# One stream of max units across the blocks of a context attention, its first phase rebuilt, and a lag of two chunks before the probabilities are weighed

## The chip, the cores and the metric

The kernel runs on one core of one Trainium2 chip. The metric is the device time in microseconds of one execution. TensorE (PE) does matrix products into PSUM, VectorE (DVE) and ScalarE (ACT) read PSUM and SBUF, GpSimd (POOL) works on SBUF, and SyncE (SP) issues most DMAs. The engines run on their own and wait for each other through semaphores.

## What is computed

A decoder of two layers on 1024 tokens (8 tiles of 128) of width 128 and a context of 6404 rows. Layer 0 is a state-space mixer (mamba), an attention of 16 heads of size 8 over the context, and a mixture of experts; layer 1 is a self-attention, a second attention over the context and another mixture of experts. After each comes a residual and a layer norm. The change is in layer 0, in its first two parts and the norm between them. The part of the reference that matters most:

```python
def _L0_xattn_ref(q, kv, mem, w_q, w_kv, w_concat):
    B, L, D = q.shape
    c = jnp.concatenate([mem, kv], axis=1)
    qh = (q @ w_q).reshape(B, L, N_HEAD, D_HEAD).transpose(0, 2, 1, 3)
    kvp = c @ w_kv
    k, v = (kvp[..., :D_HEAD], kvp[..., D_HEAD:])
    attn_score = jnp.einsum('bhid,bjd->bhij', qh, k) / np.sqrt(D_HEAD)
    attn_prob = jax.nn.softmax(attn_score, axis=-1)
    out = jnp.einsum('bhij,bjd->bhid', attn_prob, v)
    ...
x = _layernorm(x + _L0_attn_ref(x, ...))            # the mixer
x = _layernorm(x + _L0_xattn_ref(x, ctx_1024, ...)) # the context attention
```

All heads share the keys and values (6404 rows of 8 numbers each), and `softmax` needs for every query the maximum over the 6404 scores.

## The kernel before, in words

`context_attention` works in `NB` = 16 blocks. A block is 8 heads of one tile of 128 tokens, so 1024 queries. Keys are split into parts whose products sum to the wanted precision, and stand in `key_stack` twice, in partitions 0 to 63 and 64 to 127; the queries of even blocks stand in partitions 0 to 63 of `q_stack`, those of odd blocks in 64 to 127. `rows(blk)` picks the half. So a product of block b uses 64 rows of the PE array, the lower or the upper ones by the parity of b.

Each block goes through two passes. The first finds the maxima: 56 **max units** (`UNITS`, 8 heads by 7 ranges of keys). A unit is one or two matmuls of 64 x 512 (line 802; the seventh range of a head is one matmul of 260 columns) into one of two places of `max_ps`, and a reduce on DVE (`maximum`, line 959) that frees the place (`unit_used`). When all units of a block are reduced, `negate` makes two parts of the negated maxima, `turn_shift` turns them on PE (8 transposes, line 815), and a cast writes them as two further rows of `q_stack` (line 971, on DVE); that sets `q_ready`. The second pass goes over 51 **chunks** of 128 keys (`NCH`): two score matmuls (line 922; the shift is in them) into one of three banks, two exponentials on ACT (`exponentiate`, line 950) into `probs`, three deep, and `weigh` on PE (line 903), which multiplies a chunk's probabilities with the values into `acc_ps`. A block's sum is copied by ACT (`take_acc`, line 940) before the next block's first `weigh`.

The order on PE is written out by hand in `attend`. While block b goes through its chunks, PE works off the max units of block b+1, of the other parity:

```python
if with_max and c <= LAST:          # LAST = 46: one unit behind the scores of chunks 0 to 46
    max_unit(pe, blk + 1, u)
weigh(pe, blk, c - 1)               # the chunk before
if with_max and c in after_weighing:  # 9 more: behind chunks 4, 9, 14, 19, 25, 30, 35, 40, 46
    max_unit(pe, blk + 1, u)
if with_max and c == NCH - 2: turn_shift(pe, blk + 1)
```

Before block 0 there is a first phase: 16 query products (line 832), split by ACT and DVE (lines 837 and 841), the 56 max units of block 0, and 27 jobs that make layer 1's keys and values (lines 875 and 880). Ahead of that, in `mamba`, PE also makes the keys and the values of the context (`ContextKeys`): keys are `make` (line 350), values are `values` (line 359, 51 products with 8 columns each, 12 near the start and 39 later), and `take_values` copies them on DVE. `residual_norm` stands between mixer and attention: DVE normalizes, PE transposes 8 tiles (line 196), ACT copies them to `x_T`.

Of the kernel before, what the change touches and what calls it, by code (L numbers as in the profile page):

```python
# [23 lines left out]
P = 128  # L24
# [74 lines left out]
def load_and_constants(k):  # L99
# [8 lines left out]
    k.half_sel_q = k.sb("half_sel_q", [P, 1])  # L108
    k.steps = Chain(None, k.sem("vector_step"))
# [7 lines left out]
    with nc.Block() as block:  # L117
# [8 lines left out]
        def _(dve):  # L126
# [9 lines left out]
            for lo in (TERMS, P // 2 + TERMS):  # L136
                nc.vector.memset(k.half_sel[lo:lo + 32, :], 1.0)
                nc.vector.memset(k.shift_one[lo:lo + 32, :], 1.0)
            nc.vector.tensor_copy(k.ident_b[:], k.ident[:]).then_inc(k.consts_ready, 1)


def residual_norm(k, tag, branch, added=False, store=None, turned=None):
# [5 lines left out]
    with ExitStack() as tmp:  # L148
# [11 lines left out]
        with nc.Block() as block:  # L160
# [21 lines left out]
            def _(act):  # L182
# [101 lines left out]
class ContextKeys:  # L284
# [10 lines left out]
    def __init__(self, k, banks):  # L295
# [6 lines left out]
        self.v_ready, self.v_taken = k.sem("ctx_v_ready"), k.sem("ctx_v_taken")  # L302
# [49 lines left out]
    def values(self, pe, w_kv, chunks):  # L352

        nc, k = self.k.nc, self.k
        for c in chunks:
            n = P if c < NCH - 1 else TAIL
            if c in (0, self.CUT):
                pe.wait_ge(self.ctx_loaded[1 if c else 0], 16)
            ins = nc.tensor.matmul(self.v_ps[0:n, c, :], k.ctx_T[:, c * P:c * P + n], w_kv[:, HD:2 * HD], start=True,
                                   stop=True)  # L360
        if NCH - 1 in chunks:
            ins.then_inc(self.v_ready, 1)
# [36 lines left out]
def mamba(k):  # L399
# [8 lines left out]
    with ctx:  # L408
# [87 lines left out]
        with nc.Block() as block:  # L496
# [54 lines left out]
            def _(pe):  # L551
# [7 lines left out]
                keys.values(pe, w_kv, range(0, 12))  # L559
# [23 lines left out]
                keys.values(pe, w_kv, range(12, NCH))  # L583
# [3 lines left out]
                pe.wait_ge(keys.v_taken, 1)  # L587
# [72 lines left out]
            def _(dve):  # L660
# [36 lines left out]
                keys.take_values(dve)  # L697
# [27 lines left out]
        residual_norm(k, "norm0", out_ps, turned=wide(4))  # L725
# [20 lines left out]
def context_attention(k):  # L746
# [5 lines left out]

# [12 lines left out]
    with ctx:  # L765
        q_stack = k.sb("q_stack", [SPAN2, NT, BLK], F32R, ctx)
        gathered = k.sb("gathered", [P, NB, QUART], F32, ctx)
        w_out = k.params.x0_w_concat
        with ExitStack() as tmp:

            probs = k.sb("probs", [P, 3, BLK], F32, tmp)
            partial = k.sb("max_partial", [P, HB, NR], F32, tmp)
            neg = k.sb("neg_max", [P, HB], F32, tmp)
            part2 = k.sb("neg_part", [P, HB, 2], F32R, tmp)
# [3 lines left out]
            shift_ps = max_ps[:, 0, :]  # L778
            q_made, q_high, q_done = k.sem("q_made"), k.sem("q_high"), k.sem("q_done")
# [7 lines left out]

            def rows(blk):

                lo = HALF_P * (blk % 2)  # L790
                return slice(lo, lo + HALF_P)

            def max_half(pe, blk, u, a):

                h, r = u // NR, u % NR
                c0, cols = RANGES[r]
                n = min(HALF, cols - a)
                if a == 0 and not (blk == 0 and u < 2):
                    pe.wait_ge(unit_used, blk * UNITS + u - 1)
                if n <= 0:  # L800
                    return
                ins = nc.tensor.matmul(max_ps[:, u % 2, a:a + n], q_stack[rows(blk), blk // 2, h * P:(h + 1) * P],  # L802
                                       k.key_stack[rows(blk), c0 + a:c0 + a + n], start=True, stop=True)
                if a + n == cols:
                    ins.then_inc(unit_ready, 1)
# [29 lines left out]
            def high_queries(act, i):  # L835
                act.wait_ge(q_made, i + 1)
                nc.scalar.copy(q_rows(i), q_bank(i).rearrange("p (t c) -> p t c", t=4)).then_inc(q_high, 1)

            def halve_queries(dve, i):
                dve.wait_ge(q_high, i + 1)  # L840
                nc.vector.scalar_tensor_tensor(out=q_rows(i), in0=q_rows(i).bitcast(F32), scalar=k.half_sel_q[0:SPAN2, :],
                                               in1=q_bank(i).rearrange("p (t c) -> p t c", t=4), op0=ALU.mult,
                                               op1=ALU.add).then_inc(q_done, 1)
# [8 lines left out]
            FIRST_JOB = 8  # L852
# [10 lines left out]
            def queries_at(u):  # L863

                if u < 8:
                    return range(4 + u // 2, 5 + u // 2) if u % 2 == 0 else range(0)
                return range(HB + (u - 8) // 5, HB + (u - 8) // 5 + 1) if u % 5 == 3 and u < 8 + 5 * HB else range(0)
# [39 lines left out]


# [1350 lines left out]
```

## Time and profile before

| | |
|---|---|
| median of 3 runs | 2247.23 us (2247.16 to 2249.95) |
| the profiled execution: time, span | 2255.29 us, 2253.6 us |
| busy in the span: PE, DVE, ACT | 2100.2, 1590.2, 1319.3 us |
| mixer, up to its last matmul | 0 to 185.1 us |
| norm | 185.4 to 193.4 us |
| first phase of the attention | 193.4 to 306.8 us |
| the 16 blocks | 306.8 to 1432 us |

The stages overlap little, so each is read by itself. In the 16 blocks nearly every microsecond has a matmul in it; whether PE is at its pace there is read from the starts of successive matmuls, not from its busy share.

### The profile page before, as it was taken

How to read it: one execution, taken by the hardware profiler on the slowest of the kernel's cores; microseconds unless marked ns; L12 is line 12 of the kernel's file. 1: busy time of each engine (PE TensorE's matmuls, PEld its weight loads, DVE VectorE, ACT ScalarE, POOL GpSimd, SP SyncE). 2: the span in 40 equal slices, each digit the busy share in tenths (PEclk: the TensorE clock that was granted, in tenths of full speed). 3: DMA queues.
4: the chain of work that ended last, by engine and by line, in shares of the span. 5: the costliest groups of instructions: out<-in, count | busy, mean ns of one | idle time of the engine just before them, and what ended most of it. 6: DMA issues, size and time to landing. Idle time of an engine off the chain costs nothing. (4 is left out here: it accounts for less than half of the span.)

```text
span 2253.6 us, 38636 instructions
## 1 busy us (share of the span) xinstructions
PE 2100.2 (93%) x15240; PEld 995.6 (44%) x15240; DVE 1590.2 (71%) x2158; ACT 1319.3 (59%) x2189; POOL 120.0 (5%) x156
## 2 busy tenths in 40 slices
PE   8777999999999999999999999899589997999898
PEld 5223343333333333333333333477533333777755
DVE  4997578898888988889888882223778873444335
ACT  4232157777777777777777778533247773333421
POOL 1560000000000000000000000000200010000000
PEclk7898599999999999999999999899779999999989
DMA  4110000000000000000000000011000000000011
GB/s 135 56 65 0 0 1 1 1 1 1 1 1 1 1 1 1 1 1 1 1 1 1 1 1 1 13 33 35 1 1 1 0 0 0 1 1 0 1 33 33
DMA packets 22978, 24.59 MB, mean 11 GB/s; under 512 B 5728, under 2 KB 20224, under 8 KB 22576
## 3 DMA queue, kind: packets, MB, share of 16 engines
q1 hardware_dynamic: 21648, 20.44, 3.0%
q8 instruction: 104, 1.70, 0.3%
q10 hardware_dynamic: 1184, 2.10, 0.2%
q14 instruction: 42, 0.34, 0.1%
HBM read 21.81 MB, written 0.59 MB: 10 GB/s over the span
## 5 line engine op out<-in xcount | busy, mean ns | idle before, releaser
L959 DVE TENSOR_REDUCE sb_max_partial<-ps_max_ps 128x1 f32<-128x1024 f32 (+1 forms) x896 | 958.1, 1107 | 110.1 <-PE ps_max_ps L802 104.4
L950 ACT ACTIVATE sb_probs<-ps_score_ps 128x512 f32<-128x512 f32 (+1 forms) x1632 | 885.3, 595 | 237.9 <-PE ps_score_ps L922 195.2
L802 PE MATMUL ps_max_ps<-sb_key_stack,sb_q_stack 64*128 64x512 f32 (+1 forms) x1664 | 608.5, 443 | 21.7 <-DVE sb_max_partial L959 9.1
L922 PE MATMUL ps_score_ps<-sb_q_stack,sb_key_stack 64*128 64x512 f32 x1632 | 592.5, 442 | 1.9 <-issue 0.4
L903 PE MATMUL ps_acc_ps<-sb_probs,sb_val_ones 128*32 128x256 f32 x6528 | 521.4, 391 | 0.9 <-ACT sb_probs L950 0.4
L922 PEld LDWEIGHTS ps_score_ps<-sb_q_stack,sb_key_stack 64*128 64x128 f32 x1632 | 241.0, 185 | 281.1 <-ACT sb_probs L950 266.3
L802 PEld LDWEIGHTS ps_max_ps<-sb_key_stack,sb_q_stack 64*128 64x128 f32 x1664 | 256.9, 188 | 159.1 <-DVE sb_max_partial L959 135.3
L903 PEld LDWEIGHTS ps_acc_ps<-sb_probs,sb_val_ones 128*32 128x32 f32 x6528 | 128.4, 108 | 293.0 <-ACT sb_probs L950 218.6
L1654 DVE TENSOR_REDUCE sb_s_max_partial<-ps_s_max_ps 128x1 f32<-128x512 f32 x256 | 170.2, 690 | 42.5 <-PE ps_s_max_ps L1579 35.7
L1644 ACT ACTIVATE sb_s_probs<-ps_s_score_ps 128x1024 f32<-128x1024 f32 x128 | 131.0, 1024 | 49.0 <-PE ps_s_score_ps L1616 46.6
L1871 DVE TENSOR_SCALAR_CACHE_REDUCE sb_x_scores<-ps_x_score_ps 128x1024 f32<-128x1024 f32 (+1 forms) x56 | 62.1, 1111 | 80.7 <-PE ps_x_score_ps L1812 80.7
L1579 PE MATMUL ps_s_max_ps<-sb_s_k_stack_T,sb_s_q_stack_T 128*128 (+1 forms) x256 | 104.0, 408 | 6.7 <-DVE sb_s_max_partial L1654 2.8
L1839 PE MATMUL ps_x_acc_ps<-sb_val,sb_x_turned 128*128 128x128 f32 (+1 forms) x816 | 109.1, 277 | 1.2 <-DVE sb_x_turned L1851 0.9
L1812 PE MATMUL ps_x_score_ps<-sb_key_T,sb_x_q_buf 128*128 128x512 f32 (+1 forms) x208 | 99.6, 581 | 8.8 <-DVE sb_x_q_buf L1880 8.8
L1851 ACT COPY sb_x_turned<-ps_x_turn_ps 128x512 f32<-128x512 f32 (+1 forms) x52 | 29.6, 569 | 132.0 <-PE ps_x_turn_ps L1827 132.0
L1839 PEld LDWEIGHTS ps_x_acc_ps<-sb_val,sb_x_turned 128*128 128x128 f32 (+1 forms) x816 | 99.5, 191 | 3.5 <-issue 1.0
L1229 DVE SCALAR_TENSOR_TENSOR sb_e_acc<-ps_e_out_ps,sb_e_gates,sb_e_acc 128x128 f32<-128x128 f32 x136 | 36.7, 343 | 79.7 <-PE ps_e_out_ps L1209 79.7
L655 ACT ACTIVATE sb_val<-sb_delta,sb_a_neg 128x1024 f32<-128x1024 f32 x32 | 36.6, 1148 | 91.5 <-DVE sb_key_T L713 71.9
L483 PE MATMUL ps_mamba_ps<-sb_xpad,sb_ident 128*128 128x512 f32 x128 | 68.6, 661 | 22.2 <-POOL sb_xpad L548 22.2
L1218 ACT ACTIVATE sb_e_hidden<-ps_e_hid_ps,sb_e_b 128x1024 f32<-128x1024 f32 x34 | 37.7, 1112 | 78.9 <-PE ps_e_hid_ps L1198 78.9
L1597 PE MATMUL ps_s_acc_ps<-sb_s_probs,sb_s_v_buf 128*32 128x256 f32 x1024 | 82.2, 393 | 1.4 <-ACT sb_s_probs L1644 1.1
L548 POOL TENSOR_TENSOR sb_xpad<-sb_key_T,sb_val 128x1024 f32<-128x1024 f32 x31 | 73.9, 2383 | 75.7 <-DVE sb_key_T L713 72.6
(279 smaller groups left out, 1738.7 us busy)
## 6 DMA issues: line engine op xcount, KB each, us to landing
sb_val<-c_rows SPq DMA_DIRECT2D x16, 512.0 KB, 3.7
sb_e_w<-L_ffn_rW SPq DMA_DIRECT2D x30, 128.0 KB, 2.0
sb_e_w<-L_ffn_W_T SPq DMA_DIRECT2D x24, 128.0 KB, 2.1
sb_ctx_T<-ctx_T SPq DMA_DIRECT2D x1, 1664.0 KB, 7.8
sb_ctx_T<-ctx_T ACTq DMA_DIRECT2D x1, 1538.0 KB, 8.7
sb_x_T<-x_T SPq DMA_DIRECT2D x1, 512.0 KB, 4.0
sb_x_tok<-x ACTq DMA_DIRECT2D x1, 512.0 KB, 11.0
sb_e_w<-L_ffn_sW SPq DMA_DIRECT2D x4, 128.0 KB, 3.7
```

Of the source, the lines that this page charges most:

```text
L548: nc.gpsimd.tensor_tensor(read[:, s, :], state[:, s, :], c_all[:, n % DEPTH, :], ALU.mult).then_inc(read_ready, 1)
L802: ins = nc.tensor.matmul(max_ps[:, u % 2, a:a + n], q_stack[rows(blk), blk // 2, h * P:(h + 1) * P], k.key_stack[rows(blk), c0 + a:c0 + a ...
L903: ins = nc.tensor.matmul(acc_ps[32 * q:32 * q + 32, 0:QUART], k.val_ones[:, v, :], probs[:, v % 3, q * QUART:(q + 1) * QUART], start=(v == ...
L922: nc.tensor.matmul(score_ps[:, e % 3, :], k.key_stack[rows(blk), c * P:(c + 1) * P], q_stack[rows(blk), blk // 2, j * HALF:(j + 1) * HALF] ...
L950: nc.scalar.activation(probs[0:n, c % 3, j * HALF:(j + 1) * HALF], score_ps[0:n, e % 3, :], ACT.Exp).then_inc(exp_done, 1)
L959: nc.vector.tensor_reduce(partial[:, h, r:r + 1], max_ps[:, u % 2, 0:RANGES[r][1]], AX.X, ALU.max).then_inc(unit_used, 1)
L1579: nc.tensor.matmul(max_ps[:, u % 2, :].rearrange("p (t c) -> p t c", t=4), block_of(q_T, h, u // 2), half_of(k_T, h, u % 2), start=True, s ...
L1597: ins = nc.tensor.matmul(acc_ps[32 * j:32 * j + 32, 0:QUART], v_buf[:, s, v, :], probs[:, v % 2, j * QUART:(j + 1) * QUART], start=(v == 0 ...
L1644: nc.scalar.activation(probs[:, c % 2, :], score_ps[:, c % 2, :], ACT.Exp).then_inc(exp_done, 1)
L1654: nc.vector.tensor_reduce(partial[:, u // 2, u % 2:u % 2 + 1], max_ps[:, u % 2, :], AX.X, ALU.max).then_inc(unit_used, 1)
L1812: ins = nc.tensor.matmul(score_ps[:, local % 2, (g % 2) * HALF:(g % 2) * HALF + n], q_buf[:, s, :], k.key1_T[:, g * HALF:g * HALF + n], st ...
L1839: ins = nc.tensor.matmul(acc_ps[:, s, 0:D], turned[0:keys, local % 2, j * P:(j + 1) * P], k.val1[0:keys, c0 + j, :], start=(c0 + j == 0), ...
```

## The change

Five things are changed together. (1) The max units of all blocks form one stream, `order`, each with its `place` in the two-deep `max_ps`; it runs ahead of the blocks, so that two units of block b+2 stand before the shift of block b+1, which now comes at chunk 46 and not 49, and further ones of block b+2 in chunks 46 to 50. (2) The cast of the shift is on ACT (`take_shift`), behind the exponentials of the chunk after. (3) `weigh` takes the chunk two back (`LAG`), not one. (4) In the first phase PE subtracts the high part of the queries (`subtract_high`, with the matrix `minus_low`) and ACT copies twice; DVE does maxima alone; the units of block 0 multiply 128 rows, from `q_first`, a copy that GpSimd makes and whose upper half is zero. (5) The context's values are made and copied in the norm and no longer in `mamba`.

```diff
 class ContextKeys / mamba
-    def values(self, pe, w_kv, chunks):   # two calls in mamba: range(0, 12) and range(12, NCH)
+    def values(self, pe, w_kv):           # all 51, from residual_norm: on_pe(pe) ahead of its transposes
...
-                pe.wait_ge(keys.v_taken, 1)
-                keys.take_values(dve)
...
-        residual_norm(k, "norm0", out_ps, turned=wide(4))
+        residual_norm(k, "norm0", out_ps, turned=wide(4), on_pe=lambda pe: keys.values(pe, w_kv), on_act=keys.take_values)
 context_attention
+            FEW = 2
+            LAG = 2
+            order = [(0, u) for u in range(UNITS)] + [(0, None)]
+            for b in range(1, NB):
+                order += [(b, u) for u in range(UNITS)]
+                if b > 1:
+                    order.insert(len(order) - UNITS + FEW, (b - 1, None))
+            order.append((NB - 1, None))
+            place = {x: i for i, x in enumerate(order)}
...
+            SHIFT_AT = 46
+            lead = place[(1, None)] - FIRST + 1
+            for i, x in enumerate(order[FIRST:]):
+                if i < lead:
+                    chunk_of[x] = i * SHIFT_AT // (lead - 1)
+                else:
+                    chunk_of[x] = SHIFT_AT + (i - lead + 1) * NCH // (UNITS + 1)
...
+            def free_place(pe, item):
+                if place[item] < 2:
+                    return
+                blk, u = order[place[item] - 2]
+                if u is None:
+                    pe.wait_ge(q_ready, blk + 1)
+                else:
+                    pe.wait_ge(unit_used, blk * UNITS + u + 1)
...
+                    for item in items[:1]:
+                        issue(pe, item)
+                    if c >= LAG:
+                        weigh(pe, blk, c - LAG)
                     elif blk > 0:
-                        weigh(pe, blk - 1, NCH - 1)
+                        weigh(pe, blk - 1, NCH - LAG + c)
+                    for item in items[1:]:
+                        issue(pe, item)
...
+            def take_shift(act, blk):
+                act.wait_ge(shift_turned, blk + 1)
+                lo = HALF_P * (blk % 2) + TERMS
+                nc.scalar.copy(q_stack[lo:lo + 2, blk // 2, :], max_ps[0:2, place[(blk, None)] % 2, :]).then_inc(q_ready, 1)
...
+                    if blk < NB - 1 and blk * NCH + c == chunk_of[(blk + 1, None)] + 1:
+                        take_shift(act, blk + 1)
...
+            def subtract_high(pe, i):
+                pe.wait_ge(q_high, i + 1)
+                nc.tensor.matmul(q_bank(i), k.minus_low[:], q_rows(i), start=False, stop=True,
+                                 skip_group_check=True).then_inc(q_minus, 1)
```

What the table gives can be counted from these lines. In blocks 1 to 13 chunk c holds one item each, but two in chunks 3, 12, 20, 29, 37 (of the other parity; in chunks 20 and 37 the first of the two is a unit of 260 columns) and in chunk 46 (the shift and a unit). Units of the same parity as the block that goes through its chunks are the seven in chunks 44 to 50: six of 1024 columns and one of 260. Block 0 holds 64 items, two of the other parity in twelve chunks. Block 14 has the five doubled chunks and the shift in chunk 44; block 15 has none.

On PE, chunk 47 of block 0 and its neighbours stood so before (line 922 scores, 903 weighing, 815 the shift, 802 max units):

```order
L922 MATMUL ps_score_ps<-sb_q_stack,sb_key_stack 128x512 [waits exp_done] x2
L903 MATMUL ps_acc_ps<-sb_probs,sb_val_ones 32x256 [waits exp_done]
L903 MATMUL ps_acc_ps<-sb_probs,sb_val_ones 32x256 x3
L815 MATMUL ps_max_ps<-sb_ident,sb_neg_part 2x128 [waits neg_parts_ready]
L815 MATMUL ps_max_ps<-sb_ident,sb_neg_part 2x128 x7
L922 MATMUL ps_score_ps<-sb_q_stack,sb_key_stack 128x512 [waits exp_done] x2
```

With the change chunks 46 to 48 are these (line 954 scores, 941 weighing, 845 the shift, 836 max units, here those of block 2):

```order
L954 MATMUL ps_score_ps<-sb_q_stack,sb_key_stack 128x512 [waits exp_done] x2
L845 MATMUL ps_max_ps<-sb_ident,sb_neg_part 2x128 [waits neg_parts_ready,max_used]
L845 MATMUL ps_max_ps<-sb_ident,sb_neg_part 2x128 x7
L941 MATMUL ps_acc_ps<-sb_probs,sb_val_ones 32x256 [waits exp_done]
L941 MATMUL ps_acc_ps<-sb_probs,sb_val_ones 32x256 x3
L836 MATMUL ps_max_ps<-sb_key_stack,sb_q_stack 128x512 [waits max_used]
L836 MATMUL ps_max_ps<-sb_key_stack,sb_q_stack 128x512
L954 MATMUL ps_score_ps<-sb_q_stack,sb_key_stack 128x512 [waits exp_done] x2
L836 MATMUL ps_max_ps<-sb_key_stack,sb_q_stack 128x512 [waits q_block_ready]
L836 MATMUL ps_max_ps<-sb_key_stack,sb_q_stack 128x512
L941 MATMUL ps_acc_ps<-sb_probs,sb_val_ones 32x256 [waits exp_done]
L941 MATMUL ps_acc_ps<-sb_probs,sb_val_ones 32x256 x3
```

A unit now stands in each of these chunks, and the one of chunk 47 waits for `q_block_ready`, since the shift had its place in `max_ps`. On ACT the cast that sets it (line 974) has come in between the exponentials (line 984) of chunks 47 and 48:

```order
L984 ACTIVATE sb_probs<-ps_score_ps 128x512 [waits score_ready,pv_done]
L984 ACTIVATE sb_probs<-ps_score_ps 128x512 [waits score_ready]
L974 CAST sb_q_stack<-ps_max_ps 2x1024 [waits shift_turned]
L984 ACTIVATE sb_probs<-ps_score_ps 128x512 [waits score_ready,pv_done]
L984 ACTIVATE sb_probs<-ps_score_ps 128x512 [waits score_ready]
```

It stood on DVE before, and exponentials alone stood there on ACT. In `mamba`, these rows of PE stood between the last key product and the first product of the scan:

```order
L350 MATMUL ps_mamba_ps<-sb_ctx_T,sb_wk_rep 128x512 [waits ctx_k_done]
L359 MATMUL ps_mamba_ps<-sb_w_kv,sb_ctx_T 128x8 x14
L359 MATMUL ps_mamba_ps<-sb_w_kv,sb_ctx_T 128x8 [waits ctx_loaded1]
L359 MATMUL ps_mamba_ps<-sb_w_kv,sb_ctx_T 128x8 x23
L359 MATMUL ps_mamba_ps<-sb_w_kv,sb_ctx_T 4x8
L472 MATMUL ps_mamba_ps<-sb_b_rows,sb_b_ones 128x512 [waits ctx_v_taken,ctx_k_done,b_rows_moved,w_rep_ready]
```

The 39 values products and the wait for their copy are gone from there; all 51 stand in the norm, ahead of its transposes.

## Rows read from the trace of the kernel before

**Rows 1.** Windows: stretch, its length, busy per engine (count), PEclk, DMA share, GB/s.
```profile
40.00:54.00 14.00, 13.43 (x65) 13.30 (x64) 0.53 (x2) 0.49 (x1) 0.00 (x0) 0.50 0.00 0
185.00:189.40 4.40, 0.07 (x1) 0.00 (x0) 3.84 (x19) 1.28 (x1) 0.00 (x0) 1.00 0.00 0
189.50:199.60 10.10, 8.39 (x16) 4.00 (x17) 3.85 (x12) 4.32 (x7) 0.00 (x0) 0.50 0.00 1
199.70:216.70 17.00, 13.45 (x35) 5.07 (x33) 15.91 (x18) 3.51 (x6) 0.00 (x0) 1.00 0.00 0
216.80:223.50 6.70, 6.70 (x12) 3.03 (x11) 3.11 (x4) 1.75 (x3) 0.00 (x0) 0.50 0.00 0
...
233.90:284.90 51.00, 49.34 (x83) 21.08 (x83) 26.62 (x26) 8.22 (x15) 0.00 (x0) 0.50 0.00 0
...
304.50:375.40 70.90, 69.28 (x612) 27.45 (x611) 61.61 (x60) 54.85 (x103) 0.00 (x0) 1.00 0.01 1
```

**Rows 2.** Timeline of PE, a usual chunk of block 7: start, us, what.
```profile
804.56 0.64 PE L903 MATMUL ps_acc_ps<-sb_probs,sb_val_ones 128*32 128x256 f32 x8
805.12 0.50 PE L922 MATMUL ps_score_ps<-sb_q_stack,sb_key_stack 64*128 64x512 f32 x1
805.13 0.50 PE L802 MATMUL ps_max_ps<-sb_key_stack,sb_q_stack 64*128 64x512 f32 x1
805.47 0.39 PE L922 MATMUL ps_score_ps<-sb_q_stack,sb_key_stack 64*128 64x512 f32 x1
...
805.80 0.42 PE L903 MATMUL ps_acc_ps<-sb_probs,sb_val_ones 128*32 128x256 f32 x4
```

**Rows 3.** Windows, most of block 15, which has no max units.
```profile
1370.95:1432.10 61.15, 60.73 (x500) 22.39 (x500) 0.00 (x0) 54.04 (x100) 0.00 (x0) 1.00 0.00 1
```

**Rows 4.** Timeline of PE, block 14, around a unit behind a weighing.
```profile
1340.71 0.50 PE L802 MATMUL ps_max_ps<-sb_key_stack,sb_q_stack 64*128 64x512 f32 x1
...
1341.55 0.73 PE L802 MATMUL ps_max_ps<-sb_key_stack,sb_q_stack 64*128 64x512 f32 x2
1342.21 0.42 PE L903 MATMUL ps_acc_ps<-sb_probs,sb_val_ones 128*32 128x256 f32 x4
```

**Rows 5.** Timeline of PE at the shift of block 7.
```profile
800.22 1.03 PE L815 MATMUL ps_max_ps<-sb_ident,sb_neg_part 128*2 128x128 f32 x8
801.18 0.72 PE L922 MATMUL ps_score_ps<-sb_q_stack,sb_key_stack 64*128 64x512 f32 x2
```

**Rows 6.** Line 971, the cast of the shift: durations in ns, first and last start.
```profile
L971 DVE CAST sb_q_stack<-ps_max_ps x16: 1214/1216/1218, 304.5 to 1367.7; 2x1024 fp32r<-2x1024 f32 x16
```

**Rows 7.** Timeline of ACT: four exponentials in a row, and a copy of 1024 columns.
```profile
805.72 2.32 ACT L950 ACTIVATE sb_probs<-ps_score_ps 128x512 f32<-128x512 f32 x4 [0.23 <-PE ps_score_ps L922]
...
10.98 1.01 ACT L625 COPY sb_xpad<-ps_mamba_ps 128x1024 f32<-128x1024 f32 x1 [1.61 <-PE ps_mamba_ps L555]
```

**Rows 8.** Timeline of the mixer: the values, two records to a product, and DVE.
```profile
16.48 2.74 PE L359 MATMUL ps_mamba_ps<-sb_w_kv,sb_ctx_T 128*128 128x8 f32 x24
...
37.08 16.35 PE L359 MATMUL ps_mamba_ps<-sb_w_kv,sb_ctx_T 128*128 128x8 f32 x78
...
38.25 0.75 DVE L374 SCALAR_TENSOR_TENSOR sb_key_stack<-sb_key_stack,sb_half_sel,ps_mamba_ps 128x512 fp32r<-128x512 f32 x1
53.47 0.57 DVE L386 COPY sb_val_ones<-ps_mamba_ps 128x400 f32<-128x400 f32 x1 [14.48 <-PE ps_mamba_ps L359]
...
54.04 1.20 DVE L704 TENSOR_TENSOR sb_delta<-sb_delta,sb_key_T 128x1024 f32<-128x1024 f32 x1
```

**Rows 9.** Timeline of PE in the norm.
```profile
190.29 2.26 PE L196 MATMUL ps_mamba_ps<-sb_ident,sb_x_tok 128*128 128x128 f32 x8 [5.22 <-DVE sb_x_tok L178]
```

**Rows 10.** Timeline of PE in the first phase, ahead of a fall and in slow time.
```profile
215.08 0.73 PE L802 MATMUL ps_max_ps<-sb_key_stack,sb_q_stack 64*128 64x512 f32 x2 [1.47 <-DVE sb_max_partial L959]
...
239.17 1.22 PE L802 MATMUL ps_max_ps<-sb_key_stack,sb_q_stack 64*128 64x512 f32 x2
```

**Rows 11.** Line 841, DVE's share of the query split.
```profile
L841 DVE SCALAR_TENSOR_TENSOR sb_q_stack<-sb_q_stack,sb_half_sel_q,ps_score_ps x14: 734/747/748, 196.2 to 285.3; 128x512 fp32r<-128x512 f32 x14
```

More of the change, by code:

```diff
@@ L791, in rows, with max_unit @@
                 return slice(lo, lo + HALF_P)
-            def max_half(pe, blk, u, a):
+            def free_place(pe, item):
[6 more added lines that the diff above has]
+                    pe.wait_ge(unit_used, blk * UNITS + u + 1)
+            def max_unit(pe, blk, u):
                 h, r = u // NR, u % NR
                 c0, cols = RANGES[r]
[L797 to L805, printed above, removed]
@@ L807, in max_unit @@
-            def max_unit(pe, blk, u):
-                for a in (0, HALF):
-                    max_half(pe, blk, u, a)
+                free_place(pe, (blk, u))
+                for a in range(0, cols, HALF):
+                    n = min(HALF, cols - a)
+                    dst = max_ps[:, place[(blk, u)] % 2, a:a + n]
+                    if blk == 0:
+                        ins = nc.tensor.matmul(dst, q_first[:, h * P:(h + 1) * P], k.key_stack[:, c0 + a:c0 + a + n],
+                                               start=True, stop=True)
+                    else:
+                        ins = nc.tensor.matmul(dst, q_stack[rows(blk), blk // 2, h * P:(h + 1) * P],
+                                               k.key_stack[rows(blk), c0 + a:c0 + a + n], start=True, stop=True)
@@ L861, in jobs_at @@
                 return range(early * (u - FIRST_JOB) // of, early * (u + 1 - FIRST_JOB) // of)
[L863 to L867, printed above, removed]
+            EARLY = 3
+            MADE_AT = {0: 3, 2: 4, 4: 5, 6: 6, 8: 7, **{11 + 5 * i: HB + i for i in range(HB)}}
+            MINUS_AT = {0: 2, 1: 3, 3: 4, 5: 5, 7: 6, 9: 7, **{12 + 5 * i: HB + i for i in range(HB)}}
             def layer1_job(pe, i):
@@ L997, in _ @@
                     for blk in range(NB):
-                        attend(pe, blk, blk < NB - 1)
-                    weigh(pe, NB - 1, NCH - 1)
+                        attend(pe, blk)
+                    for v in range(NCH - LAG, NCH):
+                        weigh(pe, NB - 1, v)
                 @block.scalar
@@ L1015, in _ @@
                     take_acc(act, NB - 1)
+                @block.gpsimd
+                def _(pool):
+                    nc.gpsimd.memset(q_first[HALF_P:P, :].bitcast(F32), 0.0)
+                    for h in range(HB):
+                        pool.wait_ge(q_done, h + 1)
+                        nc.gpsimd.tensor_copy(q_first[0:HALF_P, h * P:(h + 1) * P],
+                                              q_stack[0:HALF_P, 0, h * P:(h + 1) * P].bitcast(F32)).then_inc(first_ready, 1)
                 @block.vector
```

145 lines of the change are left out of this document (73 added, 72 removed).

## The prediction

> **What bounds the kernel now.** I read the stages one by one, from the windows, then the timeline in the places that the change touches.
>
> In the 16 blocks the windows show PE busy for 69.28 of 70.90 us, DVE 61.61 and ACT 54.85 [rows 1]. The timeline says more. From one weighing to the next a usual chunk takes 805.80 - 804.56 = 1.24 us. In it the max unit starts with the first score matmul, 0.01 us behind, and the second score matmul starts 0.35 us later [rows 2]. A unit uses the other 64 rows of the array and costs nothing. Block 15 has no units, and its 50 chunks take 61.15 us, 1.22 each [rows 3]: the pace is that of two scores and a weighing. A unit that has no scores beside it pays: behind a weighing at 1340.71 a unit goes with the next scores, so the chunk's own stands alone at 1341.55, and the weighing starts 0.66 us after it; without it it would have started at 1341.37, so 0.84 us are lost, 0.18 of them to DVE [rows 4]. The shift takes 801.18 - 800.22 = 0.96 us [rows 5]. Check: casts of the shift are (1367.7 - 304.5) / 15 = 70.88 us apart [rows 6], and 51 x 1.24 + 8 x 0.84 + 0.96 = 70.9. (The ninth unit behind a weighing is short and has free scores beside it.) So PE sets the pace. DVE's idle time, 9 us a block, is no cost.
>
> Before the blocks, three things stand out. DVE waits 14.48 us for 39 products with 8 columns, 78 records in 16.35 us [rows 8], at the lower clock of 1.2 GHz (0.50) [rows 1]. In the norm PE idles 5.22 us before its transposes [rows 9]. In the first phase the clock is at 1.2 GHz from 216.8 to 223.5 and from 233.9 to 284.9 [rows 1].
>
> **Mixer.** DVE is done at 39.0 and goes on at 54.04 [rows 8]. With the products gone it goes on at once: -15.0 us. The 12 earlier products, 2.74 us [rows 8], come while ACT and DVE still make what PE needs next, and count nothing; if they did, -2.7 more.
>
> **Norm.** All 51 products stand ahead of the transposes, which ACT's copies and then the whole next stage wait for. At 2.4 GHz a product takes 2.74 / 12 = 0.228 us, at 1.2 GHz 16.35 / 39 = 0.419 [rows 8]. Against an idle time of 5.2 us [rows 9] that is 51 x 0.228 - 5.2 = +6.4 at best and 51 x 0.419 - 5.2 = +16.2 at worst. Before, the clock held for the 4.4 us after the mixer and then fell [rows 1]; products of 8 columns kept it low in the mixer [rows 1, 8]. So I take 4.4 us fast (19 products) and 32 x 0.419 = 13.4 slow: 17.8 - 5.2 = +12.6. ACT's copy of the values is added at the stage's end; by DVE's 0.57 for it [rows 8] and a small second one, +0.7.
>
> **First phase.** 57.7 us of it run at 1.2 GHz [rows 1]. A unit alone takes 1.22 us there against 0.73 [rows 10], a ratio of 1.67. At full clock that work is 34.6 us: -23.1, with DVE's 26.62 + 3.11 still under it. DVE loses 16 splits of 0.747 us [rows 11]; they count only where DVE is the pace, in the 17 us at 2.4 GHz in which it is busy for 15.91 [rows 1], about six of them: -4.5. PE gains 16 subtractions; at a 512-column score's 0.35 [rows 2] that is +5.6. Sum -22. It hangs on the clock: the units now fill all 128 rows, and DVE holds PE up less. Were it as low as before, only -4.5 and 5.6 to 9 (at the ratio) would remain, +1 to +5; were PE never held up either, some 10 us more would go, -32.
> The rows show no price for going from 64-row to 128-row matmuls: score to score is 0.35 us, score to weighing 0.33 [rows 2]. The Trainium skill, TensorEngine Tiling (Array Packing), Key Properties, says that a change of tiling mode drains TensorE, and its page TensorE: Matmul & The Clock Gate, Part 2, gives a drain as about 128 cycles. By that the full-row units of block 0 would save some 86 switches of 0.05 us, an estimate of 4 us from those pages; the sum below would be 2331 by it. The trace does not bear it out, and it is left out.
>
> **Blocks.** The lag of two chunks: the weighing's place in the order gives ACT one more chunk of slack, but it is not waited for now, so 0. What stays per block is 51 x 1.24 = 63.2. Five chunks have two units: 3 x 0.84 + 2 x 0.66 (a short one first) = 3.8 instead of 6.7. But seven units now use the same 64 rows as the scores beside them, so they follow one another: 6 x 0.66 + 0.3 = 4.3 more. The shift is 0.96 as before. And the unit in chunk 47 waits for ACT's cast. From the start of the scores ACT needs 0.60 us to begin, 2 x 0.58 for two exponentials [rows 2, 7], then the cast: 1.01 by ACT's copy of 1024 columns [rows 7], 1.22 by DVE's cast of the same tile [rows 6]. With 0.1 for the way back the unit starts 2.9 us after the scores and not 0.66: 2.2 lost (2.4 with the longer cast). Behind it on PE stand the weighing of chunk 45 and the scores of chunk 48, which ACT then waits for; nothing covers it. Sum 63.2 + 3.8 + 4.3 + 0.96 + 2.2 = 74.5, +3.6 a block. Thirteen blocks (1 to 13): +47. Block 0 has seven doubled chunks more, 7 x 0.84 = 5.9: +9.5. Block 14 is 63.2 + 3.8 + 0.96 = 68.0: -2.9. Together +54. The floor of the wait is 0, if ACT's cast were early, which its place behind chunk 47's exponentials excludes.
>
> **The clock at the wait.** In the blocks PE never stood still, and the clock never left 2.4 GHz [rows 1, 3]. In the first phase it fell at 216.7, when PE had been held up for 1.47 us at 215.08 [rows 10]. Now it is held up for 2.2 us, 14 times, among matmuls that use half the rows. I take it that it falls. The shortest time at 1.2 GHz was 6.7 us, the usual one 10.1, the longest 51.0 [rows 1]; in 10.1 us PE does 10.1 / 1.67 = 6.0 us of work, 4.1 lost. 14 x 4.1 = +57.
>
> **Sum.** -15.0 + 12.6 + 0.7 - 22 + 54 = +30; with the clock +87. The differences come from one execution of 2255.3 us; the median is 2247.2, 0.4% less, which changes a sum of this size by 0.3 us. 2247.2 + 87 = **2335 us**.
>
> **Rivals.**
> A, the forecast: the clock falls at most waits, 2335; by itself 2295 (half as many falls, a better first phase) to 2385 (each lasts 15 us). 0.52.
> B, the clock holds: 2247 + 30 = 2277. For it: 2.2 us is not long, and a weighing follows 0.7 us behind. Against it: the fall after 1.47. 0.30.
> C, faster: the pace of a chunk is not PE's but that of the chain exponential, weighing, score, exponential, which the lag of two opens. ACT needs 2.32 / 2 = 1.16 a chunk [rows 7]. At best 816 x 0.08 = 65 less than B, 2212; it decides below a pace of 1.20, where the 30 us are made good. For it: ACT is idle 0.23 us before its row. Against: where ACT is far ahead, in the doubled chunk, the matmuls follow one another in the same 0.66 [rows 4]. 0.10.
> D, the clock stays down across blocks, as it did for 51 us [rows 1]: PE's 74.5 us become 124. If it does for half of the time, 15 x 25 = +370, 2650. Against it: the usual chunk fills all rows. 0.06.
> E, first phase and norm at their best, 10 and 6 us less, and a wait that half hides (-15): 2247. 0.02.
>
> **Numbers.** A measurement tells 0.2%, 4.5 us, from no change. C is faster, 0.10; E and a tail of B the same, 0.03; the rest slower, 0.87. The range takes in B with its better ends and A up to 2385, and leaves out C and D: 2260 to 2385.
>
> **What would show it.** The casts on ACT: 74.5 us apart if the clock holds, 78 to 79 with falls. Idle time of some 2.2 us on PE before line 836, released by `sb_q_stack`. PEclk under 1.0 behind chunk 47. Unit and score matmuls of chunks 44 to 50 in a row, not side by side. The first phase down to 91 us at 1.0, the norm up from 8 to 21 us, the mixer's last matmul at 170. I am wrong if the pace in chunks 5 to 11 is under 1.20, if PE is not held up at chunk 47, or if same-row units run beside the scores.

## The result, and the profile after

The changed kernel takes 2331.38 us (median of 4 runs, 2328.49 to 2332.97) against 2248.59 us for the kernel before beside it: a ratio of 1.0359, 95% interval 1.033 to 1.0387. It is slower by 83 us; the prediction said 87. The profiled execution of the changed kernel took 2332.97 us with a span of 2330.8 us and a mean granted clock of 0.928; that of the kernel before took 2255.3 us with a span of 2253.6 us and a clock of 0.952. It was 7 us above the kernel's median, so the two traces lie 77 us apart and not 83.

By stage, from the two traces: the mixer's last matmul ends at 172.3 us instead of 185.1 (-12.7); the norm takes 21.5 instead of 8.4 us (+13.1); the first phase 79.0 instead of 113.3 (-34.3); the blocks, first score to last weighing, 1236.5 instead of 1125.9 (+110.5). The sum is +76.6; the two spans differ by 77.2. So everything ahead of the blocks got 34 us faster and the blocks 110 us slower.

Windows of the profile after, from the norm into the blocks, with one fall of the clock early and one late (columns as in [rows 1]):

```profile
176.70:197.10 20.40, 19.05 (x81) 16.82 (x80) 2.34 (x9) 3.65 (x7) 0.95 (x1) 0.50 0.00 1
197.20:270.00 72.80, 65.89 (x269) 40.73 (x268) 59.58 (x59) 31.67 (x55) 2.29 (x8) 1.00 0.00 0
270.40:347.30 76.90, 71.91 (x600) 29.52 (x600) 64.31 (x63) 55.11 (x101) 0.00 (x0) 1.00 0.01 1
347.40:357.50 10.10, 10.10 (x49) 4.06 (x49) 4.37 (x5) 4.32 (x8) 0.00 (x0) 0.50 0.00 0
...
893.00:896.80 3.80, 1.92 (x13) 1.03 (x14) 1.80 (x2) 1.90 (x4) 0.00 (x0) 1.00 0.00 0
896.90:907.10 10.20, 10.20 (x49) 3.79 (x47) 4.11 (x4) 4.27 (x9) 0.00 (x0) 0.50 0.00 0
907.20:971.90 64.70, 62.99 (x563) 25.22 (x561) 56.06 (x54) 51.43 (x96) 0.00 (x0) 1.00 0.01 1
```

The first phase, which ran at 1.2 GHz for 57.7 us in [rows 1], now has 1.00 from 197.2 on. In the blocks, where it never left 1.00, it falls to 0.50 in every block that has a wait: 14 times, for 10 or 14 us each. The wait itself, in the timeline of the changed kernel, chunk 47 of one block:

```profile
893.22 0.59 ACT L984 ACTIVATE sb_probs<-ps_score_ps 128x512 f32<-128x512 f32 x1
893.83 1.00 ACT L974 CAST sb_q_stack<-ps_max_ps 2x1024 fp32r<-2x1024 f32 x1
894.88 0.73 PE L836 MATMUL ps_max_ps<-sb_key_stack,sb_q_stack 64*128 64x512 f32 x2 [2.02 <-ACT sb_q_stack L974]
895.55 0.64 PE L941 MATMUL ps_acc_ps<-sb_probs,sb_val_ones 128*32 128x256 f32 x8
...
896.70 0.88 PE L836 MATMUL ps_max_ps<-sb_key_stack,sb_q_stack 64*128 64x512 f32 x2
...
897.51 1.08 PE L941 MATMUL ps_acc_ps<-sb_probs,sb_val_ones 128*32 128x256 f32 x8
```

The unit (L836, 802 before) stands 2.02 us until the cast is there, and 2 us after it has gone on, at 896.9, the clock falls: the same eight weighing records take 0.64 us at 895.55 and 1.08 us at 897.51. The views of the cast's line and of the group of line 836 count it:

```profile
L974 ACT CAST sb_q_stack<-ps_max_ps x16: 999/1000/1003, 270.4 to 1439.4; 2x1024 fp32r<-2x1024 f32 x16
...
  PE ps_max_ps L836: 28.3, 14
```

14 waits, 28.3 us, 2.02 each. From weighing to weighing blocks 1 to 13 take 78.5 us on average, 70.8 before. The values stand ahead of the transposes, as the timeline of the norm shows (before: [rows 9]):

```profile
172.66 17.94 PE L363 MATMUL ps_mamba_ps<-sb_w_kv,sb_ctx_T 128*128 128x8 f32 x102 [0.33 <-PEq L499]
190.53 1.97 PE L202 MATMUL ps_mamba_ps<-sb_ident,sb_x_tok 128*128 128x128 f32 x8
```

### The profile page after: what moved, and what is told of

It is laid out like the page before. It is cut to its first block and busy times, and to the rows that moved or that the text cites. A ratio compares the mean times of both kernels' runs of the same rounds, so it can differ in the third digit from the quotient of the medians.

```text
span 2330.8 us, 38707 instructions
## 1 busy us (share of the span) xinstructions
PE 2161.0 (93%) x15256; PEld 1040.9 (45%) x15256; DVE 1571.6 (67%) x2125; ACT 1346.0 (58%) x2223; POOL 122.7 (5%) x165
## 5 line engine op out<-in xcount | busy, mean ns | idle before, releaser
L995 DVE TENSOR_REDUCE sb_max_partial<-ps_max_ps 128x1 f32<-128x1024 f32 (+1 forms) x896 | 969.8, 1108 | 276.4 <-PE ps_max_ps L836 242.4
L954 PE MATMUL ps_score_ps<-sb_q_stack,sb_key_stack 64*128 64x512 f32 x1632 | 620.8, 461 | 0.8 <-ACT sb_probs L984 0.4
L836 PE MATMUL ps_max_ps<-sb_key_stack,sb_q_stack 64*128 64x512 f32 (+1 forms) x1560 | 581.4, 450 | 35.5 <-ACT sb_q_stack L974 28.3
L941 PE MATMUL ps_acc_ps<-sb_probs,sb_val_ones 128*32 128x256 f32 x6528 | 550.2, 411 | 0.2
L954 PEld LDWEIGHTS ps_score_ps<-sb_q_stack,sb_key_stack 64*128 64x128 f32 x1632 | 254.6, 194 | 325.3 <-ACT sb_probs L984 281.6
L836 PEld LDWEIGHTS ps_max_ps<-sb_key_stack,sb_q_stack 64*128 64x128 f32 x1560 | 255.8, 195 | 117.4 <-DVE sb_max_partial L995 60.4
L1693 ACT ACTIVATE sb_s_probs<-ps_s_score_ps 128x1024 f32<-128x1024 f32 x128 | 131.0, 1024 | 49.2 <-PE ps_s_score_ps L1665 46.7
L1665 PE MATMUL ps_s_score_ps<-sb_s_q_stack_T,sb_s_k_stack_T 128*128 (+1 forms) x256 | 77.6, 385 | 0.0
```

The costliest lines, as they stand in the source:

```text
L836: ins = nc.tensor.matmul(dst, q_stack[rows(blk), blk // 2, h * P:(h + 1) * P], k.key_stack[rows(blk), c0 + a:c0 + a + n], start=True, stop ...
L941: ins = nc.tensor.matmul(acc_ps[32 * q:32 * q + 32, 0:QUART], k.val_ones[:, v, :], probs[:, v % 3, q * QUART:(q + 1) * QUART], start=(v == ...
L954: nc.tensor.matmul(score_ps[:, e % 3, :], k.key_stack[rows(blk), c * P:(c + 1) * P], q_stack[rows(blk), blk // 2, j * HALF:(j + 1) * HALF] ...
L995: nc.vector.tensor_reduce(partial[:, blk % 2, h, r:r + 1], max_ps[:, place[(blk, u)] % 2, 0:RANGES[r][1]], AX.X, ALU.max).then_inc(unit_us ...
L1665: ins = nc.tensor.matmul(score_ps[:, c % 2, half * HALF:(half + 1) * HALF].rearrange("p (t c) -> p t c", t=4), block_of(k_T, h, c), half_o ...
L1693: nc.scalar.activation(probs[:, c % 2, :], score_ps[:, c % 2, :], ACT.Exp).then_inc(exp_done, 1)
```

## The experiments

Theory A: the hold-up of 2 us at ScalarE's cast makes the clock fall, and both together are the loss. Its rivals: S, the same-row units, which leave half of the array idle, bring the falls; C, the lag of two is worth something; F, that the full-row units of the first phase keep its clock up, and G, that VectorE holding TensorE up less does so. Diffs are against the changed kernel unless another is named.

**1. cast_on_vector.** The stream stays; the cast goes to VectorE, where it stands behind the next block's second unit.

```diff
-                    if blk < NB - 1 and blk * NCH + c == chunk_of[(blk + 1, None)] + 1:
-                        take_shift(act, blk + 1)
...
                         for u in range(UNITS):
+                            if u == FEW and blk > 1:
+                                take_shift(dve, blk - 1, nc.vector.tensor_copy)
                             maximum(dve, blk, u)
```

> The changed kernel, but VectorE takes the shift of blocks 1 to 15 behind the second unit of the next block, instead of ScalarE behind chunk 47. The stream of units, the seven same-row units and the lag of two stay. Theory A (the hold-up of 2.0 us makes the clock fall, and that costs some 4.2 us more): the hold-up at chunk 47 goes, the clock stays at 1.00 in all blocks, casts 72 us apart instead of 78.4, 2331 - 14 x 6.3 = 2243 us. Rival S (the same-row units, which leave half of the array's rows idle, make the clock fall): the falls stay, only the 2.0 us go, 2331 - 28 = 2303 us.

2224.2 us (2222.07 to 2226.44), ratio 0.9923 [0.9896, 0.995]: 0.8% below the kernel before, a small difference, but the interval ends short of 1. All blocks in one window:

```profile
272.00:1399.00 1127.00, 1120.37 (x9822) 453.05 (x9818) 932.48 (x898) 884.69 (x1641) 0.00 (x0) 1.00 0.01 1
```

The clock stays at 1.00 and blocks 1 to 13 take 71.0 us. Rival S falls: the same-row units alone bring no fall. The wait and what followed it were worth 78.5 - 71.0 = 7.5 us a block, where 6.3 was expected; over all blocks that is 104.8 us. The mixer also ended 4.9 us earlier than in the first trace (167.4 for 172.3), which is a difference from run to run (see the end).

**2. stream_held_back.** No same-row units and no wait; the cast stays on ScalarE.

```diff
+            for x in order[FIRST:]:
+                chunk_of[x] = (x[0] - 1) * NCH + (48 if x[1] is None else x[1] * 47 // UNITS)
```

(with `FEW = 0`.)

> The changed kernel, but the units of block b run in chunks 0 to 46 of block b - 1 alone, its shift in chunk 48 and ScalarE's cast behind chunk 49, as before the change: no same-row units, and nothing waits for the cast. Lag of two, first phase and norm stay as changed. Theory A: the clock never falls in the blocks, 70.9 us each as before, 1125 us of blocks instead of 1236: 2331 - 110 = 2221 us, faster than the kernel before by 1.2%. Rival C (the lag of two opens the pace): under 2190 us, usual chunks under 1.20 us. Rival L (the lag costs something): over 2235 us.

2240.76 us (2238.2 to 2243.66), ratio 0.9985 [0.9963, 1.0008]. No fall in the blocks, as A said, but they take 72.3 to 72.6 us, not 70.9, and the time missed 2221 by 20 us. It is even over the 2235 that rival L (the lag costs something) named; run 7 settles L. Usual chunks are at 1.24, so rival C is out. The excess lies in two chunks of 2.14 and 2.11 us around the cast, and the expectation "nothing waits for the cast" was wrong. The view of the cast's line (L971 here) names the next block's first scores (L951):

```profile
who waited for it (us, times):
  PEld ps_score_ps L951: 10.9, 15
  PE ps_score_ps L951: 3.7, 15
```

In the timeline of one block the cast runs from 845.54 to 846.54, the scores that wait for it start at 846.60, and the unit that usually runs beside them starts only at 847.21. Run 6 takes that up. These waits of 0.25 us brought no fall.

**3. hold_up_alone.** The held-back stream, and TensorE waits in one chunk of each block for a copy on ScalarE.

```diff
+            HOLD_AT = [20] * 8 + [48] * 7 + [99]
+            HOLD_COLUMNS = [1024, 1024, 512, 512, 256, 256, 64, 64] + [1024] * 8
...
+                    if c == HOLD_AT[blk]:
+                        pe.wait_ge(held_up, blk + 1)
```

> The held-back stream, in which TensorE is made to wait behind the scores of one chunk of each block for a copy that ScalarE makes behind that chunk's exponentials (the copy's result is not used). Blocks 0 to 7: in chunk 20, beside usual units, with copies of 1024, 1024, 512, 512, 256, 256, 64 and 64 columns; blocks 8 to 14: in chunk 48, with 1024 columns and no unit near. Hold-ups of about 2.2, 1.7, 1.5 and 1.3 us. Theory A: each long hold-up is followed by 10 to 14 us at 0.50 though there is no same-row unit; if at all 15, 2221 + 29 + 15 x 4.2 = 2313 us; the short ones may be spared. Rival S (the same-row units are needed for a fall): 2221 + 29 = 2250 us, clock 1.00 in all blocks.

2302.26 us, one execution. The hold-ups measured 1.91, 1.49, 1.28 and 1.12 us in chunk 20 (two blocks each) and 1.92 us in chunk 48. The timeline at the first and at a short hold-up:

```profile
299.11 1.03 ACT L990 COPY sb_idle_copy<-sb_q_stack 2x1024 f32<-2x1024 f32 x1
300.18 1.22 PE L836 MATMUL ps_max_ps<-sb_key_stack,sb_q_stack 64*128 64x512 f32 x2 [1.91 <-ACT sb_idle_copy L990]
...
766.76 0.72 PE L836 MATMUL ps_max_ps<-sb_key_stack,sb_q_stack 64*128 64x512 f32 x2 [1.12 <-ACT sb_idle_copy L990]
```

The window behind the first:

```profile
299.80:310.00 10.20, 9.82 (x49) 3.79 (x51) 5.20 (x5) 3.59 (x7) 0.00 (x0) 0.50 0.00 0
```

Seven of the eight hold-ups in chunk 20 were followed by 0.50, those of 1.12 us too; one of the two of 1.91 us was not. There were only usual units around, so a hold-up can be enough without same-row units, and S is refuted from this side too. In chunk 48, with 1.92 us, the shift and no unit near, three of seven were followed by 0.50, each for 3.4 us: less than A said.

**4. shorter_hold_ups.** Where is the floor? The held-back stream with VectorE's cast; the wait in chunk 20 is for exponentials of that chunk.

```diff
+            HOLD = [1] * 7 + [2] * 8 + [0]
...
+                    if c == 20 and HOLD[blk]:
+                        pe.wait_ge(exp_done, blk * EXPS + JOBS * c + HOLD[blk])
```

> The held-back stream with VectorE's cast (2226.6 us). TensorE waits in chunk 20 behind the scores for that chunk's first exponential (blocks 0 to 6, held up some 0.35 us) or for both (blocks 7 to 14, some 0.9 us). The shortest hold-up so far, 1.12 us, was followed by 0.50 for 3.4 or 10 us in both its blocks, and the one of 1.91 us in block 1 by none. Theory A with a graded effect: no falls in blocks 0 to 6, falls in at least half of blocks 7 to 14, each some 4 us: about 2226.6 + 8 + 4 x 4 = 2250 us. Rival T (only hold-ups of 1 us and over count): no fall at all, 2235 us.

2271.62 us, one execution. The hold-ups were 0.51 to 0.52 and 1.00 to 1.01 us; the first of either kind:

```profile
299.16 0.72 PE L834 MATMUL ps_max_ps<-sb_key_stack,sb_q_stack 64*128 64x512 f32 x2 [0.51 <-ACT sb_probs L984]
...
808.18 0.80 PE L834 MATMUL ps_max_ps<-sb_key_stack,sb_q_stack 64*128 64x512 f32 x2 [1.01 <-ACT sb_probs L984]
```

Windows: blocks 0 to 6, and behind the first of the longer ones:

```profile
274.00:808.60 534.60, 523.57 (x4574) 202.88 (x4573) 454.61 (x442) 409.36 (x758) 0.00 (x0) 1.00 0.01 1
808.70:818.90 10.20, 10.20 (x58) 3.67 (x57) 5.58 (x6) 4.01 (x8) 0.00 (x0) 0.50 0.01 2
```

No fall behind seven hold-ups of 0.51 us, a fall of 3.4 to 10 us behind each of eight of 1.01 us. T's forecast of no fall at all was wrong, but its limit of 1 us is not refuted: the longer hold-ups were expected at 0.9 us and came out at just over 1. What is shown is that 0.51 us was too short and 1.01 us long enough. The time is 20 us above the 2250 of theory A, since a block pays more than the hold-up. The held-up unit starts behind the scores and not beside them, so a block with 0.51 us and no fall takes some 72.6 us, against 71.4 in run 6; with 1.01 us and a fall it takes 74.3 to 77.3 us (blocks 7 to 13).

**5. cast_a_chunk_earlier.** The changed kernel, the cast one chunk earlier.

```diff
-                    if blk < NB - 1 and blk * NCH + c == chunk_of[(blk + 1, None)] + 1:
+                    if blk < NB - 1 and blk * NCH + c == chunk_of[(blk + 1, None)]:
```

> The changed kernel, with ScalarE's cast behind the exponentials of the chunk that turns the shift instead of the next one. The unit that waits for it comes a chunk later, so its hold-up all but goes; ScalarE is still 1.0 us behind once a block, which cost 0.9 us a block in the held-back stream. Theory A: the clock stays at 1.00, 71.0 + 0.9 us a block, 2331 - 14 x 6.5 = 2240 us. Rival: the hold-up moves to the scores, which wait for ScalarE's exponentials, and the clock falls as before, 2310 us or more.

2226.98 us, one execution, 13 us under A's 2240; 71.0 us a block, and 1.00 in all of them:

```profile
276.00:1404.00 1128.00, 1121.40 (x9828) 453.42 (x9828) 915.37 (x883) 900.76 (x1658) 0.00 (x0) 1.00 0.01 1
```

Line 836, which sat idle for 28.3 us on `sb_q_stack` in the changed kernel, does not name it any more:

```profile
L836 PE MATMUL ps_max_ps<-sb_key_stack,sb_q_stack 64*128 64x512 f32 (+1 forms) x1560 | 552.8, 431 | 7.1 <-DVE sb_max_partial L995 1.2
```

So 105 of the 110 us that the blocks lost (1131.4 us for them here, 1236.5 in the changed kernel) hang on the one chunk by which the cast stands too late. ScalarE's cast costs nothing here: nothing on TensorE waits for it, and it falls among the same-row chunks, which take 1.69 us each (run 8) and hold 1.16 us of exponentials.

**6. held_back_cast_on_vector.** Both edits, of run 1 and of run 2: the order of run 2, and the cast of run 1, with `FEW = 0` right behind the negation.

> The held-back stream of units, but with VectorE's cast. In that run (2240.8 us, 72.3 us a block) the two chunks around ScalarE's cast took 2.1 us each, 0.9 more than a chunk with the shift alone would explain. Theory Q (ScalarE's cast costs it 0.9 us a block, because ScalarE has 1.16 us of exponentials in a chunk of 1.24): 71.4 us a block, 2227 us. Rival R (the place of the units costs it): 72.3 us a block still, 2240 us. Beside 2224 us of the run with the stream it also prices the stream with its same-row units: within 5 us of nothing.

2226.58 us (2224.66 to 2228.25), ratio 0.9914 [0.9894, 0.9934]; 71.4 us a block, and of the two slow chunks one is left, that of the shift. The size is what theory Q said; its reason is not shown. The edit moves the cast to another engine and also makes it earlier: it starts 1.0 us after the shift begins here and some 3.2 us after it in run 2. Run 2's trace has the scores themselves waiting for the late cast, so "the cast stood too late" explains the 0.9 us without "ScalarE had no room". No run puts ScalarE's cast earlier in this order of units; run 5 does it in the other order, and there it costs nothing. Beside run 1 the stream itself is worth 2 us, less than the measurement tells.

**7. lag_of_one.** Against run 1:

```diff
-            LAG = 2
+            LAG = 1
```

> The run with VectorE's cast (2224 us, usual chunk 1.23 to 1.24 us), in which a chunk's probabilities are weighed one chunk later instead of two. Theory N (the lag is worth nothing, PE sets the pace): usual chunks 1.24 us, 2221 to 2228 us. Rival C (the lag opens the chain of exponential, weighing and score): slower, 2240 us or more, chunks of 1.26 and above.

2225.61 us (2225.29 to 2227.24), ratio 0.991 [0.989, 0.993]; blocks 71.0 us, usual chunks 1.23 to 1.24. The lag is worth nothing either way, as far as these runs can tell; C is out, and so is L of run 2.

**8. first_units_on_64_rows.** The changed kernel with half-row units in the first phase.

```diff
-                        ins = nc.tensor.matmul(dst, q_first[:, h * P:(h + 1) * P], k.key_stack[:, c0 + a:c0 + a + n],
+                        ins = nc.tensor.matmul(dst, q_first[0:HALF_P, h * P:(h + 1) * P], k.key_stack[0:HALF_P, c0 + a:c0 + a + n],
```

> The changed kernel, but the units of block 0 use 64 of the array's 128 rows in the first phase, not all. Same results, same waits. Theory F (full-row units hold the clock up there): the clock is at 0.50 for tens of us again, the first phase takes over 95 us instead of 79, and the time is 2347 us or more. Rival G (the clock holds because VectorE no longer holds TensorE up): first phase 79 us, clock 1.00 from its third microsecond, 2331 us.

2337.25 us, one execution; neither theory. The clock holds, as G said (window of the phase):

```profile
194.70:277.30 82.60, 78.31 (x285) 39.70 (x283) 60.28 (x59) 33.95 (x59) 2.29 (x8) 1.00 0.00 0
```

Yet the stretch from the last transpose to the first score is 87.6 us, and 80.3 to 80.9 in the eight traces with full-row units and the values in the norm. The timeline of this run, and then of the changed kernel, units (L833) and queries (L871) in turn:

```profile
216.54 0.73 PE L833 MATMUL ps_max_ps<-sb_key_stack,sb_q_first 64*128 64x512 f32 x2
217.20 1.12 PE L871 MATMUL ps_score_ps<-sb_x_T,sb_wq_rep 128*128 128x512 f32 x2
218.25 0.73 PE L833 MATMUL ps_max_ps<-sb_key_stack,sb_q_first 64*128 64x512 f32 x2
```

```profile
216.61 1.03 PE L833 MATMUL ps_max_ps<-sb_key_stack,sb_q_first 128*128 128x512 f32 x2
217.48 1.03 PE L871 MATMUL ps_score_ps<-sb_x_T,sb_wq_rep 128*128 128x512 f32 x2
217.94 1.03 PE L833 MATMUL ps_max_ps<-sb_key_stack,sb_q_first 128*128 128x512 f32 x2
```

A unit and a query take 1.71 us with half-row units and 1.33 with full-row ones: 0.38 us for a change from 128 to 64 rows and back. F is out. G's forecast of the clock came true, but its cause is not tested: no run gives VectorE its splits back or takes the subtraction off TensorE. Run 1 shows the same in the blocks, in two same-row chunks:

```profile
838.49 0.73 PE L954 MATMUL ps_score_ps<-sb_q_stack,sb_key_stack 64*128 64x512 f32 x2
839.06 0.62 PE L836 MATMUL ps_max_ps<-sb_key_stack,sb_q_stack 64*128 64x512 f32 x2
839.61 0.64 PE L941 MATMUL ps_acc_ps<-sb_probs,sb_val_ones 128*32 128x256 f32 x8
840.18 0.73 PE L954 MATMUL ps_score_ps<-sb_q_stack,sb_key_stack 64*128 64x512 f32 x2
```

Four half-row matmuls (two of scores, two of a unit of the same rows) run from 838.49 to the weighing at 839.61, 1.12 us, where two take 0.68 in the usual chunk (805.12 to 805.80 in [rows 2]). From scores to scores the chunk takes 840.18 - 838.49 = 1.69 us and not 1.24. A same-row unit therefore adds some 0.45 us, 0.22 to 0.23 for each matmul. By the same working the 0.35 and 0.33 of [rows 2] hold some 0.1 each for the change to 64 rows and back.

**9. values_in_mixer.** Run 1 with the values back at their old place and their copy on VectorE:

```diff
+                keys.values(pe, w_kv, range(0, 12))
...
+                keys.values(pe, w_kv, range(12, NCH))
...
+                keys.take_values(dve)
```

> The run with VectorE's cast, but the context values are made in the mixer and copied by VectorE, as before the change. By the prediction's terms (mixer +15.0, norm -13.3): 2226 us, the same as 2224 within the measurement. Rival: the norm's part is smaller because the clock is low there anyway and the mixer's full size is paid: 2230 us or more.

2222.69 us (2222.11 to 2226.09), ratio 0.9899 [0.9878, 0.992]: the same as run 1 within the measurement. In the traces the mixer ends 15.0 us later than in run 1 and the norm is 13.2 us shorter. The move itself is worth nothing that these runs can tell.

**10. values_as_jobs.** Run 1 with the values as the last jobs of the first phase.

```diff
+            head_jobs = [(c, min(9, NCH - 1 - c)) for c in range(0, NCH - 1, 9)] + [(NCH - 1, 1)]
+            JOBS1 = len(key_jobs) + len(val_jobs) + len(head_jobs)
```

> The run with VectorE's cast, but the 51 context value products are neither in the mixer nor in the norm: they go in seven groups, each copied by ScalarE, to the end of the list of jobs that TensorE works off between the units of the first phase, where the clock is at 1.00. Norm: -13.3 us (18 us of products at 1.2 GHz less the 5 us hidden). Theory P (TensorE is the bound of the first phase): the products cost 51 x 0.228 = 11.6 us there, 2222 us. Rival V (VectorE's maxima are, and TensorE's idle time there takes them in): 2211 us.

2227.36 us (2224.39 to 2230.87), ratio 0.992 [0.9896, 0.9944]. The norm gave 13 us back, the first phase took 11 of them, by a way that neither theory had, and the blocks took 5 more (1136.6 us against 1131.7 in run 1; the low clock lasts until 274.6, into block 0). Windows of the phase:

```profile
179.00:250.60 71.60, 68.89 (x312) 46.28 (x310) 60.08 (x59) 33.15 (x59) 2.29 (x8) 1.00 0.00 1
250.70:266.70 16.00, 15.71 (x79) 15.01 (x78) 0.00 (x0) 2.16 (x7) 0.00 (x0) 0.50 0.00 0
```

TensorE is busy 15.71 of 16.00 us behind 250.7, and still the clock is at 0.50; it does little else there than 8-column products.

**11. values_between_jobs.** The same products, at most four at a time, between layer 1 jobs.

```diff
+            head_jobs = list(val_jobs)
...
+            mixed = sorted((j / n, s + j) for s, n in zip(starts, (len(key_jobs), len(val_jobs), len(head_jobs))) for j in range(n))
```

> In the run with the values as seven jobs at the end of the first phase the clock fell at 250.7 us, when TensorE did little but 8-column products, and the phase grew by what the norm gave back. Here the products go in 14 groups of at most four, each between two layer 1 jobs, so that none stands beside another. Theory H (the products make the clock fall only where they stand in a row): clock 1.00 up to the first scores, first phase 80.5 + 51 x 0.228 = 92 us at most or 86 where VectorE's pace hides half, 2213 to 2219 us. Rival W (they lower it wherever they stand, or cost TensorE what they saved): 2224 to 2228 us.

2218.35 us (2216.35 to 2220.3), ratio 0.987 [0.9836, 0.9904], the lowest median, 1.3% below the kernel before; its interval still overlaps those of runs 1, 6, 7, 9 and 10. The first phase's window:

```profile
183.70:265.50 81.80, 77.77 (x397) 55.52 (x396) 63.56 (x62) 38.23 (x77) 2.03 (x7) 1.00 0.00 1
```

1.00 until the blocks' first chunk. Theory H holds: the stretch from the last transpose to the first score is 84.9 us, where it is 79.8 without any products (run 9) and 91.6 with them at its end (run 10). The 51 products cost 5 us there, 0.1 each.

## Why the prediction was right, step by step

The mechanism, a wait for ScalarE's cast in chunk 47 that also costs the clock, was right: runs 1 and 5 take the wait away by different means, and both win back 105 of the 110 us that the blocks lost; runs 3 and 4 bring falls back with a hold-up alone. That the total came within 4 us is luck in part. Its terms were read from a trace that was 7 us above the median, and from trace to trace they should have made 87 us where 77 were measured. And within the blocks two large errors cancel: the forecast was 17 us too high without the wait and 19 us too low for the clock.

- **Mixer, forecast -15.0, measured -12.7.** The step was right: in runs 1 and 2 VectorE goes on at 39.2 us, forecast 39.0. In the changed kernel's trace it goes on at 41.3; the clock had fallen there at 29.9 instead of 32.4. Run 9, which puts the products back, ends its mixer 15.0 us later than run 1.
- **Norm, +13.3, measured +13.1.** The step was right: the products took 17.94 us, forecast 17.8.
- **First phase, -22, measured -34.3**, outside the step's own range of -32. The step that failed is "The trace does not bear it out, and it is left out", on the change of tiling: the full-row units are worth 7 us (run 8). The 0.35 us from score to score, read as a price without a change, already held one, since the first score follows a weighing. The Trainium skill, TensorEngine Tiling (Array Packing), Key Properties, says that changing the tiling mode drains TensorE. Run 8 agrees in so far as such a change costs time; that it is a drain can't be seen there. The measured 0.38 us for two changes is larger than two of the 0.05 us that the prediction estimated from the 128 cycles of the Trainium skill, TensorE: Matmul & The Clock Gate, Part 2. The other 5 us are not tested. The case "were PE never held up either" explains 2.4 of them at most: in the first phase TensorE was idle 9.1 us before the units in the kernel before and still 6.7 us in the changed one, and the prediction had counted a part of that as DVE's -4.5. A further microsecond or so lies in the start of the phase, which was at 0.50 up to 199.6 before and up to 197.2 now.
- **Blocks without wait, +23 (54 less 14 waits of 2.2), measured +5.7** (run 1: 1131.7 against 1125.9). The step that failed is the same-row unit at 0.66 us; it takes 0.45. Six of them make 1.3 us, as much as the block of 74.5 - 2.2 = 72.3 was too long against 71.0.
- **Wait, 2.2 us, measured 2.02.**
- **Clock, 4.1 us a fall, measured 5.5** (7.5 less the wait, with whatever ScalarE's late exponentials cost). Both parts of the term were too small. The falls lasted 12.2 us on average, not 10.1. And the ratio of 1.67, read from a unit alone, is 1.73 for a usual chunk, which takes 2.15 us from weighing to weighing at 0.50 and 1.24 at 1.00:

```profile
905.06 1.08 PE L941 MATMUL ps_acc_ps<-sb_probs,sb_val_ones 128*32 128x256 f32 x8
...
907.21 0.64 PE L941 MATMUL ps_acc_ps<-sb_probs,sb_val_ones 128*32 128x256 f32 x8
```

  Together they make 12.2 x (1 - 1 / 1.73) = 5.2.
- Rival B, that the clock holds, is refuted by the 14 falls. C is refuted by run 7. D, that the clock stays down across blocks, never came: each fall ended after 10 or 14 us. Of E the better first phase came, the half-hidden wait did not. S, which the prediction hinted at with "among matmuls that use half the rows", is no cause by itself.

Open stays why one hold-up of 1.91 us was followed by no fall, why those in chunk 48 had short ones or none, and what keeps the clock of the first phase up.

## What to carry to other kernels

Where TensorE in a full stream waits for another engine, price the wait with the clock that it may take down: 2 us of waiting cost 7.5 us here, 0.5 us cost 1.2 us and no clock, and one chunk in the producer's place decided 104 us. A spacing of two matmuls read from a trace has in it what stood between them: before it is used as the price of one more, see whether the two share the same rows.

## What was not expected of the hardware

- Hold-ups of only 1.01 us in an otherwise full stream were each followed by 3.4 to 10 us at 0.50 (8 of 8), those of 0.51 us by none (0 of 7, run 4).
- TensorE can be busy 15.71 of 16.00 us and be granted 0.50, with 8-column products (run 10). The same products between others left it at 1.00 and cost 0.1 us each (run 11); in the norm they took 0.35 us each (17.94 / 51).
- A change from 128-row to 64-row matmuls and back costs 0.38 us (run 8).
- The same program's mixer ended between 167.4 and 172.3 us in the eleven traces that have it. The clock's falls in its first 60 us came at different times, and the two latest ends (172.2 and 172.3) are those of the earliest first falls (29.7 and 29.9). A single profile can't tell 5 us there.
